# A graph-attention layer on one core: new preface, halves order, products one unit behind, SyncE's last store, one of eight units copied by VectorE

## The reference

```python
h  = jnp.maximum(_layernorm(x, axis=-1), 0.0)        # x: (8192, 64) float32, eps 1e-5
Wh = h @ W                                           # W: (64, 64)
e  = (Wh @ a1)[:, None] + (Wh @ a2)[None, :]         # a1, a2: the two halves of a, 64 each
e  = jax.nn.leaky_relu(e, negative_slope=0.2)
scores    = jnp.where(adj > 0, e, -9e15)             # adj: (8192, 8192) int32, about 1 in 2048 set
attention = jax.nn.softmax(scores, axis=1)
out = x + jax.nn.elu(attention @ Wh)
```

## Time and profile before

| | us |
|---|---|
| three runs | 723.67, 724.67 (median), 726.57 |
| the profiled execution | 723.94 |
| its span, first to last instruction | 720.2 |
| busy in the span: PE, DVE, ACT, POOL | 638.5, 625.0, 633.3, 36.1 |
| mean rate of the DMAs over the span | 382 GB/s |
| mean granted TensorE clock | 0.964 |

### The profile page before, as it was taken

The page is one execution under the profiler, slowest core; times in us unless marked ns, Lnnn a source line. Parts: engine busy times, 40 slices in busy tenths (PEclk is TensorE's granted clock), DMA queues, the critical chain, the costliest instruction groups (busy, mean ns, idle before and its releaser), DMA issues.

```text
span 720.2 us, 24610 instructions
## 1 busy us (share of the span) xinstructions
PE 638.5 (89%) x10422; PEld 627.6 (87%) x10422; DVE 625.0 (87%) x640; ACT 633.3 (88%) x361; POOL 36.1 (5%) x47
## 2 busy tenths in 40 slices
PE   5753999999899998999899898989899998999891
PEld 4533999999899898989899898989899898989891
DVE  7897899999898989989898989889898989889851
ACT  5587999999899897989899897989899897989840
POOL 1000000101000010101000010000000000000000
PEclk9985999999999999999999999999999999999996
DMA  9663999999999999999999999999999999999900
GB/s 319 274 244 129 400 423 420 421 419 423 418 422 420 422 418 422 420 422 423 420 421 419 422 419 421 420 422 420 420 422 420 422 418 422 419 422 421 411 26 9
DMA packets 42882, 275.02 MB, mean 382 GB/s; under 512 B 4976, under 2 KB 9072, under 8 KB 10096
## 3 DMA queue, kind: packets, MB, share of 16 engines
q1 hardware_dynamic: 41024, 270.55, 91.1%
q0 software_dynamic: 1536, 4.20, 1.6%
q10 hardware_dynamic: 304, 0.03, 0.0%
HBM read 272.66 MB, written 2.10 MB: 382 GB/s over the span
## 4 chain that ended last, share of the span: by engine, by line
DMA 50%; DVE 19%; ACT 11%; PE 9%; issue 7%; SPq 1%; DVEq 1%; ACTq 0%; POOL 0%
DMA adj_ring<-in_adj 50%; DVE code L432 10%; ACT work L331 8%; PE psum L684 3%; PE psum L682 3%; PE psum L667 2%; DVE code L439 2%; SPq L219 1%; DVE work L445 1%; ACT work L338 1%; ACT trow L305 1%; DVE V L531 1%; DVE lows L402 1%; DVE lows L411 1%; DVE Wh L421 1%
## 5 line engine op out<-in xcount | busy, mean ns | idle before, releaser
L684 PE MATMUL psum<-V,work 128*128 128x130 f16 x4096 | 498.8, 222 | 0.0
L682 PE MATMUL psum<-V,work 128*128 128x130 f16 x4096 | 498.6, 221 | 0.0
L331 ACT ACTIVATE work<-trow,ns 128x4096 int8<-128x4096 f32 x128 | 477.1, 3727 | 0.0
L682 PEld LDWEIGHTS psum<-V,work 128*128 128x128 fp8e4 x4096 | 405.0, 99 | 0.0
L684 PEld LDWEIGHTS psum<-V,work 128*128 128x128 fp8e4 x4096 | 400.9, 98 | 0.0
L432 DVE TENSOR_SCALAR code<-adj_ring 128x4096 uint8<-128x4096 int32 x128 | 294.1, 2298 | 41.9 <-DMA adj_ring<-in_adj 40.3
L667 PE MATMUL psum<-identb,code 128*128 128x128 bf16 x2048 | 139.9, 223 | 52.8 <-DVE code L439 45.4
L667 PEld LDWEIGHTS psum<-identb,code 128*128 128x128 bf16 x2048 | 122.9, 100 | 58.0 <-DVE code L439 45.4
L439 DVE SCALAR_TENSOR_TENSOR code<-work,code 128x1024 int32<-128x1024 int32 x128 | 156.8, 1225 | 15.0 <-ACT work L331 12.6
L338 ACT COPY work<-psum 128x1024 int32<-128x1024 int32 x128 | 130.2, 1017 | 39.2 <-PE psum L667 38.4
L445 DVE TENSOR_SCALAR work<-work 128x1024 int32<-128x1024 int32 x128 | 87.9, 686 | 3.2 <-PE psum L684 3.2
(11 more groups left out here) (77 smaller groups left out, 133.5 us busy)
## 6 DMA issues: line engine op xcount, KB each, us to landing
adj_ring<-in_adj SPq DMA_DIRECT2D x256, 1024.0 KB, 15.4
work<-in_x SPq DMA_DIRECT2D x4, 512.0 KB, 6.1
xg<-in_x POOLq DMA_DIRECT2D x16, 128.0 KB, 6.0
out_y<-res POOLq DMA_DIRECT2D x16, 128.0 KB, 5.9
W<-in_L_gnn_W ACTq DMA_DIRECT2D x2, 16.0 KB, 4.4
a_sb<-in_L_gnn_a ACTq DMA_DIRECT2D x1, 0.5 KB, 5.9
```

Of the source, the lines that this page charges most:

```text
L331: nc.scalar.activation(sign[:, k % 2].bitcast(I8), trow[:, h * UW:(h + 1) * UW], ACT.Sign, bias=ns[:, B:B + 1] if isinstance(B, int) else ...
L682: nc.tensor.matmul(sums_of[:, 0:FP], up8[:, j // 2, j % 2], V[:, jb, 0:FP], start=h == 0 and j == 0, stop=False, skip_group_check=True)
L684: last = nc.tensor.matmul(sums_of[:, FP:2 * FP], down8[:, j // 2, j % 2], V[:, jb, FP:2 * FP], start=False, stop=h == 1 and j == HB - 1, s ...
```

## The change

What it does, part by part:

- **Preface.** GpSimd adds minus the mean (`xh`), ScalarE scales the row sums (`minus_means`); W is loaded twice, the second time straight into `Wx`, and the attention vectors stand ahead of it, with a sign (so that `Wh` holds -s and t, -t and a column of ones). Sqrt's and Exp's tables of ScalarE are called ahead of need by two activations on an unused word. The limits take fewer instructions; `uu` is no longer scaled by an instruction of its own but within `products`, which now has 65 columns and makes the denominators' parts too, so that the four instructions on those are gone. The scan of unit 0 stands before `products(0)`, and `V`'s rounds 2 and 3 are made inside the first body, whose first product waits only for round 0. GpSimd's first load of x waits for `V` to be complete.
- **Halves order.** A body takes the first half of the columns for its 4 blocks, then the second half for the same blocks. The pairs' sums are complete after units 5 and 7.
- **Products one unit behind.** Step k of a body: VectorE `codes(k+1)`, `find_ups(k)`, `edges(k+2)`; TensorE `transpose_unit(k+1)`, `multiply_unit(k)`. `take_sums` of the second pair and `divide` move to step 1 of the next body, `result` to step 4, `take_sums` of the first pair to step 7.
- **One copy on VectorE.** The unit 7 of each body is copied out of PSUM by VectorE (`copy_unit` in VectorE's block), after `edges` in step 6.
- **Last store.** SyncE, not GpSimd, stores the last body's result, after its last load.

```diff
@@ GpSimd
+                for b in range(NR):
+                    if b:
+                        pool.wait_ge(s_xc, b)
+                    pool.wait_ge(s_nm, b + 1)
+                    nc.gpsimd.tensor_tensor(xh[:, out_of(b)], xh[:, out_of(b)],
+                                            stat[:, 1, out_of(b)].unsqueeze(2).to_broadcast([P, RR, F]), ALU.add)\
+                        .then_inc(s_xc, 1)
...
+                pool.wait_ge(s_lo, 2 * NR)
+                x_of(0)
@@ ScalarE
-                high_parts(0)
-                act.wait_ge(s_ns, 1)
                 act.wait_ge(s_trow, 4)
                 step(0, 0)
+                high_parts(0)
                 spread(4)
                 spread(5)
+                step(0, 1)
+                copy_unit(0, 0)
                 high_parts(1)
-                step(0, 1)
                 spread(6)
                 spread(7)
-                high_parts(2)
-                high_parts(3)
...
-                        if not (last and k + 1 >= BU):
+                        if k + 1 != MINE and not (last and k + 1 >= BU):
                             copy_unit(i, k + 1)
@@ VectorE
+                def copy_unit(i, k):
...
+                    nc.vector.tensor_scalar(codeT[:, k % RC].bitcast(I32), unitT[k % 2].bitcast(I32), 0, None,
+                                            ALU.bitwise_or).then_inc(s_codeT, 1)
...
                     for k in range(BU):
-                        if not (last and k + 2 >= BU):
-                            codes(i, k + 2)
+                        if not (last and k + 1 >= BU):
+                            codes(i, k + 1)
                         find_ups(i, k)
-                        if not (last and k + 3 >= BU):
-                            edges(i, k + 3)
-                        if k == 2 and not first:
+                        if k == 1 and not first:
                             take_sums(i - 1, 1)
                             divide(i - 1)
-                        if k == 5 and not first:
+                        if k == 4 and not first:
                             result(i - 1)
-                        if k == 6:
+                        if k == 7:
                             take_sums(i, 0)
+                        if k + lead < (BU if last else BU + 2):
+                            edges(i, k + lead)
+                        if k + 1 == MINE:
+                            copy_unit(i, k + 1)
+                        if first and k == 0:
+                            products(2)
+                        if first and k == 1:
+                            low_parts(2)
+                            products(3)
+                        if first and k == 2:
+                            low_parts(3)
@@ TensorE
                     for k in range(BU):
-                        if not (last and k + 2 >= BU):
-                            transpose_unit(i, k + 2)
-                        multiply_unit(i, k)
+                        if not (last and k + 1 >= BU):
+                            transpose_unit(i, k + 1)
+                        multiply_unit(i, k, first)
@@ SyncE
+                sp.wait_ge(s_res, NI)
+                sp.dma_start(out_i[NI - 1], res[:, :, :].rearrange("p (w b) f -> p w b f", b=2)).then_inc(s_last, 16)
```

More of the change, by code:

```diff
@@ L57, in build_gat @@
     TR = 8
[L58 removed]
+    assert JB % (2 * NR) == 0 and JB % KE == 0 and 2 * F == P and HP % 2 == 0 and RT == UT * KE
     ctx = ExitStack()
@@ new lines, in _ @@
+                squares(0)
+                minus_means(2)
+                act.wait_ge(s_wp, 2)
+                for h in range(2):
+                    nc.scalar.activation(Wx[h * F:(h + 1) * F, h * FX:h * FX + 3], psum[h * F:(h + 1) * F, 7, P:P + 3],
+                                         ACT.Copy).then_inc(s_wx, 1)
+                minus_means(3)
+                copy_hT(0)
+                squares(1)
+                deviation(0)
+                copy_hT(1)
+                squares(2)
+                deviation(1)
@@ new lines, in _ @@
+                squares(3)
+                copy_hT(2)
+                deviation(2)
+                copy_hT(3)
+                spread(0)
+                deviation(3)
+                act.wait_ge(s_norm, 2)
+                nc.scalar.activation(ext[0:F, 2:3], norm2[:, :], ACT.Sqrt, scale=float(F)).then_inc(s_sq2, 1)
+                nc.scalar.activation(unused[:, 1:2], ones[:, 0:1], ACT.Exp).then_inc(s_table, 1)
+                spread(1)
+                act.wait_ge(s_lim, 1)
+                t_all = Wh[:, :, 1]
@@ L382, in body @@
                         if not (last and k + 3 >= BU):
                             step(i, k + 3)
-                        if k == 4 and not first:
+                        if k == 2 and not first:
                             negative_part(i - 1)
```

448 lines of the change are left out of this document (227 added, 221 removed).

## The result

| | before | after |
|---|---|---|
| median of the runs | 725.03 us (723.67 to 726.57, 4 runs) | 706.69 us (705.16 to 707.38, 4 runs) |
| ratio, with its 95% interval | | 0.9743 [0.9718, 0.9769] |
| profiled execution | 723.94 us | 706.51 us |
| its span | 720.2 us | 704.7 us |

The change makes the kernel 18 us faster. The forecast was 711.5, with a range from 706 to 718: the direction and the two large terms came as forecast, but 4.8 us more were gained, at the end of the program and outside the span.

A forecast was written before the change was run, and what follows sets the result against it. The adj stream was taken to bound the loop, so gains lay only in head and end: 6.9 + 5.9 + 0.3 = 13.1 us off 723.94 gives 710.8, forecast as 711.5 since the median stands 0.7 higher; range 706 to 718.

The forecast's parts named there:

- the two large terms: Stream standing still less at the start, 6.9 us off, and less work after the stream's end, 5.9 us off.
- The loop, 0 us: Steady loop: the copy and shorter lead stay hidden by the adj stream, VectorE at 37.6 of 40.5 us per body.
- GpSimd's additions: Start of the kernel: four additions moved from VectorE, taken as 2.2 us each, between 1.23 and 3.7.
- The head, 6.9 us: Start of the kernel: the stream's standstills sum to 17.6 us in place of 24.5.
- The walk through VectorE's queue: First body: step-by-step timing of VectorE's instructions, scan 0 at 27.0 us to scan 6 at 70.4.
- the limits: Before the first scan: ready at 27.0 in place of 30.1 us, 3.0 of VectorE's 5.6 us saved coming through.
- The half clock: First body: TensorE at half clock for short work at 48 to 53 and 64 to 69 us, costing it 2 us each.
- the lateness around 90 to 105 us: After the first body: copy, sums and divide make scans late again by 0 to 4.4 us; 3.2 walked.
- The tail, 5.9 us: After the stream's end: TensorE's last work ends 14.4 us behind it instead of 20.3; bounds 5 to 7 off.
- The last store, 0.3 us: End of the program: SyncE in place of GpSimd saves 0.3 us, up to 0.8 either way.
- gains less: Rival for the head: GpSimd at 3.7 us per addition, or clock falls; 716 to 718 us; 0.18 with no gain included.
- The loop loses its overlap: Rival for the loop: engines need more than 5.06 us per unit, each 0.1 us costing 12 us; chance 0.05.

The follow-up runs named there:

- e3: Changed kernel with all eight units of a body copied out of PSUM by ScalarE again; 706.22 us.
- e6: Changed kernel whose last body alone runs masks and transposes two units ahead of the products and scans three, as in the kernel before; 710.23 us.
- e2: Changed kernel with the last store given back to GpSimd; 709.98 us.
- e1: Kernel before, with the last body's result stored by SyncE and waited for there, not by GpSimd; 721.76 us against 724.53.
- e12: Changed kernel without the early call of the square root on ScalarE, so three table fetches in place of two; 706.80 us.
- e5: Changed kernel with the four centring additions given back to VectorE, the scalings by -1/64 staying on ScalarE; 707.99 us.
- e7: Changed kernel with the units of a body in the order of before (both blocks of a pair, first half, then second, then next pair); 706.25 us.
- e10: e9 plus the scan three units ahead of the product in bodies 0 to 7, two behind from body 8 on; 705.96 us.
- e4: Changed kernel with VectorE copying four of a body's eight units from the second body on, ScalarE copying one word for three of them; 719.95 us.
- e9: Changed kernel with take_sums and divide behind the scan of their unit in VectorE's queue, not ahead of it; 708.24 us.
- e11: e10 plus, in the first body, unit 3's mask and round 3's products ahead of round 2's low parts in VectorE's queue; 702.85 us.
- e8: Changed kernel with the scan three units ahead of the product in every body but the last; 705.62 us.

## Why the prediction came out as it did

- **The loop, 0 us: right.** 420 GB/s, a body of 40.5 us, VectorE at 37.75 (forecast 37.6), the copy at 1.22 us (1.2). The copy costs like an operation with a PSUM operand and not like find_ups at 0.70, as the Trainium skill, "VectorE: DVE Perf Modes", § Why PSUM operands drop a tier, has it. e3 shows that the stream hides the copy.
- **GpSimd's additions: 1.95 us each against 2.2 taken** from between 1.23 and 3.7.
- **The head, 6.9 us: 6.2 at E.** The walk through VectorE's queue was good in its steps, and late from the start: scans 0, 1, 2, 3, 4, 5 and 6 were walked at 27.0, 31.4, 39.9, 47.4, 53.5, 62.9 and 70.4 and came 1.4 to 2.3 us later. 1.4 of it is the limits, of which 3.0 us were to come through and 1.8 did (28.3 in place of 30.1): in ScalarE's queue the last root stands behind the first spread, which waited 1.68 us for TensorE, and VectorE waited 1.46 us for the root. The half clock at 46 to 53 and 63 to 70 us came where it was walked, and so did the lateness around 90 to 105 us: 3.2 in the walk, 3.4 in the table's measure from scan 6 to scan 11. Adding up pauses was the wrong sum, though. What decides is the latest scan; that is scan 3 before and scan 11 after, so 18 us won at scan 3 left 6. By that rule the walk's own scans give 52.2 - (70.4 - 30.0 + 3.2) = 8.6 us, and since they came 2.3 us late, 6.2 was left. That 6.9 lies so near is luck in part: the sum took too little for the walk, and the walk was too early.
- **The tail, 5.9 us: 6.0.** TensorE was put at a start at E - 12.5 and a last matmul at E + 14.4; it restarted at 665.47, which is E - 12.5, and ended at E + 14.5. Of the two reasons, e6 gives the lag 3.4 and leaves 2.6, for the place of the sums as is to be supposed.
- **The last store, 0.3 us: the term that was mis-sized; 3.3 measured** (e2; 2.8 in e1). I compared how the two queues issue, and took what follows the issue as equal. The earlier trace rows end at the issue; what the span still holds behind it, 10.6 us, was named in the prediction and not taken apart. The 1.5 us that a store on SyncE was feared to start late did not come: it started 0.03 us behind the result.
- **Outside the span, not priced: 1.9 us.** The sum was made against a profiled execution whose time exceeds its span by 3.7 us, and I took these as a constant. They fell to 1.8. Neither the store (e1, e2) nor the early fetch (e12), the copy (e3), the centring (e5) or the order of units (e7) brings them back; which part of the change does stays open.
- The rival "gains less" had no case in the changed kernel: GpSimd took under 2 us, and the granted clock was 1.00 in the loop and in the last body. Its second half is real all the same, since e10 shows such a fall of the clock in the last body, for 1.6 us. "The loop loses its overlap" did not come, and its price was too low: it took 12 us for each 0.1 us per unit above the stream's pace, and e4, with 0.05 us per unit above it, cost 13.3, since the engines then no longer make up what they are late from the head.

With 3.3 and 1.9 in place of 0.3, the prediction's own terms give 6.9 + 5.9 + 5.2 = 18.0 us, 705.9 for the profiled execution that took 706.51.

## What to carry to other kernels

Where a stream feeds a ring, find the one consumer step that is latest against the stream's pace: what is won ahead of it or behind it counts only down to the next latest. Time won for the stream must also reach the engine that ends last; if that engine is busy without a break, an earlier stream only makes its backlog longer. The slack of the loop is not idle either: it makes up what the start has cost. And take the end of the program apart like any other stage: the same 128 KB cost 3 us less when another queue stored them and waited for them.

## What the runs showed of the hardware

- A store of 128 KB that is the program's last work ends the span 10.6 us behind the result from GpSimd (before, e2) and 7.3 or 7.4 from SyncE (the changed kernel, e1). Of the 3.3 us between them 0.7 lie ahead of the first byte. From issue to landing the two differ by 0.3 us (2.2 against 1.9); most of the rest comes after that.
- GpSimd takes longer to issue a store of a result in the changed kernel: 2.14 us on average (15 of them, in the loop) against 0.73 in the kernel before, with as many bytes. In e2 14 of the 15 in the loop took 2.0 to 2.2 us, and the fifteenth and the last one 0.73. It costs nothing here, and no run tells its cause.
- The time outside the span is the same within 0.2 us in the runs of each kernel made from the changed one (1.7 to 1.9), and 3.6 to 4.3 us in those of the kernel before and of e1.
- TensorE's granted clock can fall to 0.50 (1.2 GHz) for some 3 us behind a wait of 2.0 us (e10, 664 to 668), and can stay at 1.00 behind the same wait (e9, e11).
- Runs of one kernel spread by 0.8 to 4 us, so that differences of about 1 us or less (e3, e7, e8, e10, e12 against the changed kernel) are not shown to be any.
